# A fused two-layer gated cross-attention block: step tables of its own for the opening, and expert weights of both kinds streamed tile by tile

## The reference, cut to what matters

```
x = x + tanh(g_x[0]) * A(layernorm(x))    # one head of 256, additive mask [8,512,1601]
x = x + tanh(g_f[0]) * B(layernorm(x))    # self-attention, top 4 of 16 heads of 64, chosen per batch
x = x + tanh(g_x[1]) * C(layernorm(x))    # 16 heads of 16 on the context, integer mask [512,1601]
x = x + tanh(g_f[1]) * D(layernorm(x))    # 8 experts, 256->1024->256, one per token:
    h = relu(x_n @ W1[e] + b1[e]);  y = h @ W2[e] + b2[e];  out = y * route_p
```

## Time and profile before

| what | us |
|---|---|
| median of the 3 runs | 3057.81 |
| lowest and highest run | 3052.07, 3067.73 |
| the profiled execution, its own time | 3067.29 |
| its span, first to last instruction | 3065.5 |

### The profile page before, as it was taken

How to read it: one execution, slowest core, us unless ns; L and a number is a source line. 1 busy time by engine, 2 the same in 40 slices (tenths; PEclk the granted TensorE clock), 3 DMA queues, 4 the chain that set the end, 5 groups by cost and what they waited for, 6 DMA issues and landing times.

```text
span 3065.5 us, 39733 instructions
## 1 busy us (share of the span) xinstructions
PE 2738.2 (89%) x13624; PEld 1286.6 (42%) x13624; DVE 1742.3 (57%) x4230; ACT 1460.1 (48%) x2922; POOL 302.8 (10%) x352
## 2 busy tenths in 40 slices
PE   5767999899999998999899999999899879968998
PEld 2433343344333433343334333433343323228998
DVE  1336566566666666667666675666666767642111
ACT  2132356544654464546554555455545655632332
POOL 1200010002000200020001000110011000002222
PEclk9878999999999999999999999999999999978999
DMA  4213231323122403231222214231323022046664
GB/s 168 88 32 106 55 96 38 102 49 108 45 84 53 124 17 101 56 102 46 79 78 78 69 39 107 65 87 38 102 57 81 17 60 61 17 135 214 225 216 144
DMA packets 182901, 263.87 MB, mean 86 GB/s; under 512 B 50037, under 2 KB 148573, under 8 KB 182694
## 3 DMA queue, kind: packets, MB, share of 16 engines
q1 hardware_dynamic: 166188, 188.99, 23.3%
q0 software_dynamic: 16512, 72.32, 6.9%
HBM read 200.36 MB, written 60.50 MB: 85 GB/s over the span
## 4 chain that ended last, share of the span: by engine, by line
PE 77%; DVE 9%; issue 5%; ACT 5%; DMA 1%; SPq 1%; POOL 0%; ACTq 0%; POOLq 0%; DVEq 0%
PE PS L1295 13%; PE PS L1251 11%; PE PS L1278 10%; DVE mxC L1752 6%; PE PS L980 6%; PE PS L955 6%; PE PS L1419 5%; PE PS L1430 4%; PE PS L1003 3%; PE PS L1139 3%; PE PS L1048 2%; PE PS L1066 2%; PE PS L1058 2%; ACT reg L878 2%; PE PS L968 2%
## 5 line engine op out<-in xcount | busy, mean ns | idle before, releaser
L878 ACT ACTIVATE reg<-PS 128x512 f32<-128x512 f32 (+1 forms) x1664 | 966.6, 597 | 1073.6 <-PE PS L1278 1067.9
L1752 DVE TENSOR_REDUCE mxC<-PS 128x1 f32<-128x400 f32 (+1 forms) x2048 | 1101.5, 570 | 615.5 <-PE PS L1251 603.0
L1251 PE MATMUL PS<-reg 96*128 96x400 bf16 (+1 forms) x2048 | 670.7, 343 | 98.9 <-DVE mxC L1752 55.5
L1278 PE MATMUL PS<-reg 99*128 99x512 bf16 (+1 forms) x1664 | 618.9, 389 | 38.1 <-ACT reg L878 33.2
L1251 PEld LDWEIGHTS PS<-reg 96*128 96x128 bf16 x2048 | 193.2, 98 | 650.4 <-DVE mxC L1752 479.8
L1295 PE MATMUL PS<-reg 128*17 128x512 f32 (+1 forms) x3328 | 446.1, 609 | 0.0
L1278 PEld LDWEIGHTS PS<-reg 99*128 99x128 bf16 (+1 forms) x1664 | 163.6, 100 | 371.6 <-ACT reg L878 230.0
L955 PE MATMUL PS<-reg 128*128 128x512 f32 (+1 forms) x512 | 219.2, 536 | 6.3 <-issue 4.0
L980 PE MATMUL PS<-reg 128*128 128x512 f32 (+1 forms) x416 | 213.6, 606 | 0.4 <-ACT reg L752 0.4
L901 ACT ACTIVATE reg<-PS,reg 128x128 f32<-128x128 f32 x312 | 89.0, 368 | 215.9 <-PE PS L1419 207.7
L1419 PEld LDWEIGHTS PS<-reg 128*128 128x128 f32 x1248 | 147.7, 194 | 3.1 <-issue 1.0
(11 more groups left out here) (214 smaller groups left out, 2567.1 us busy)
## 6 DMA issues: line engine op xcount, KB each, us to landing
reg<-in_D_W SPq DMA_DIRECT2D x47, 1024.0 KB, 5.6
reg<-in_A_mask POOLq DMA_DIRECT2D x32, 800.5 KB, 5.3
dramK<-reg SPq DMA_DIRECT2D x144, 100.0 KB
dramV<-reg SPq DMA_DIRECT2D x48, 272.0 KB, 2.1
reg<-in_ctxT POOLq DMA_DIRECT2D x8, 1601.0 KB, 9.9
reg<-in_ctx POOLq DMA_DIRECT2D x8, 1536.0 KB, 7.7
dramQ<-reg SPq DMA_DIRECT2D x96, 128.0 KB
reg<-dramQ SPq DMA_DIRECT2D x32, 384.0 KB, 6.5
```

Of the source, the lines that this page charges most:

```text
L878: act.activation(pr[u % RING][0:r, :], PS[0:r, s_bank(v), :], ACT.Exp).then_inc(a_expC, 1)
L1251: last = mm(PS[:, bank, 0:w], qs[(NG * bb + g) % 3][0:ROWS, h, t * P:(t + 1) * P], ks[g % 2][0:ROWS, h, c0:c0 + w], start=True, stop=True)
L1278: last = mm(PS[0:r, bank, :], ks[g % 2][0:STK, h, c * P:c * P + r], qs[(NG * b + g) % 3][0:STK, h, :], start=True, stop=not with_mask)
L1752: v.tensor_reduce(mxC[:, h, t, j:j + 1], PS[:, m_ring(bb, g)[i % len(m_ring(bb, g))], 0:M_CH[j][1]], AX.X, ALU.max).then_inc(v_mx, 1)
```

## The change

It has two parts.

**The opening** gets a loop of its own, `for w in range(W_END)` with 226 steps, on every engine, and the main loop starts at b = 0. The functions `prepare` and `start_next` take a plan `p` in place of the global tables: `LOOP` holds the old tables, `FIRST` those of batch 0 and `SECOND` those of stage A of batch 1. Batch 0 uses other banks: a ring of four (MB, F0, F1) for stage A's scores, two for every set of transposes (F2 and SB[0]), MB for K and SB for V projections, four (F0, F1, MB) for stage B's scores; group 0 of C's first scores of batch 0 uses a ring of four (MB, SB). Stage A of batch 0 has four mask buffers, two of them in the region of `pr`, all loaded at the start. The K and V weights are loaded first with a semaphore of their own, the other 14 weight DMAs wait until mask row block 1 has landed, and PE waits for them only in `out_a`. Two K and three V chunks are projected before the router, the other ten chunks between the router and the B projections. `gather_heads` reads the four indices in one go and issues the four large DMAs, then the four small ones. `set_mask` moves to step 40, in stage A of batch 0, and `partition_all_reduce` behind batch 1's root. Stage A of batch 1 does its first eight chunks before or right behind C's Q projection, and C's first scores come after that, two per step in 32 steps.

**Stage D** keeps no W2 in SBUF: each tile loads W1, b1, W2 (1 MB) and b2 from SP in this order into one of WB = 6 buffers, with a semaphore for W1 and b1 and one for W2 and b2. The early load of all eight W2 and the registers `chosen` go.

```
-WB = 4
+WB = 6
+FIRST = Plan(SC=49, OA=(75, 77), LB=79, XB=(86, 88), RL=92, K=[78, 80, 94, 96, 98, 99, 100, 101],
+             V=[79, 81, 82, 90, 93, 95, 97], QB=(104, 105), KB=(106, 107), VB=(108, 109), LA=0, XA=(7, 9),
+             SB=O_SB, TB=[O_SB[i // 2] + 6 + 2 * (i % 2) for i in range(16)], PVB=(O_SB[3] + 11, O_SB[7] + 11),
+             OB=(150, 151), LC=153, QG=(10, 12), XC=(161, 163), QC=(165, 167),
+             S=[14, 15, 16, 17, 18, 19, 20, 21, 26, 27, 28, 29, 34, 35, 36, 37],
+             T=[22, 23, 24, 25, 30, 31, 32, 33, 38, 39, 40, 41, 43, 44, 45, 46],
+             PV=[48 + c for c in range(2 * CT)], wrap=0, ctx=0)
+SECOND = FIRST._replace(LA=100, XA=(112, 115), QG=(153, 155),
+                        S=[168, 170, 172, 174] + [178 + 10 * t + d for t in range(3) for d in (0, 2, 4, 6)],
+                        T=[178 + 10 * t + 2 * j for t in range(QT) for j in range(4)],
+                        PV=[216 + c for c in range(sum(u < NU for u in U_PV))], ctx=180)
+W_PIECE, W_ROWS = (186, 218), 222
+W_END = 226
...
 def m_ring(bb, g):
+    if bb == 0 and g == 0:
+        return MB + SB
...
+def ring_a(n, i):
+    return (MB + (F0, F1))[i % 4] if n == 0 else (F0, F1)[i % 2]
+def turn_a_bank(n, i):
+    return (F2, SB[0])[i % 2] if n == 0 else F2
+def k_bank(n, u):
+    return (MB if n == 0 else (F0, F1))[u % 2]
+def v_bank(n, i):
+    return (SB if n == 0 else (F1, F0))[i % 2]
+def ring_b(n, i):
+    return ((F0, F1), MB)[i // 2 % 2][i % 2] if n == 0 else (F0, F1)[i % 2]
...
-        w2 = take([NE, FM, D], F32)
+        w2 = [take([FM, D], F32) for _ in range(WB)]
...
+                    (wkC[:], a["C_WkT"]...), (wvC[:], a["C_WvT"]...), (bkC[:], a["C_bk"])):
+                sp.dma_start(dst, src).then_inc(ld["k"], 16)
+            sp.wait_ge(ld["mk1"], 16)
...
-                for j in range(ACTIVE):
-                    h = sp.value_load(rti[0:1, 1, j:j + 1], min_val=0, max_val=HB - 1)
+                _, heads = nc.values_load_multi_w_load_instructions(
+                    rti[0:1, 1, 0:ACTIVE], engines=[mybir.EngineType.SP], ...)
+                for j, h in enumerate(heads):
                     sp.dma_start(ws[:, :, :, j, :], a["B_w"][bass.ds(h, 1)]...)
...
+            for w in range(W_END):
+                bring(0, w, FIRST)
+                if w == 106:
+                    load_k(0, 0, 0)
+                    load_k(0, 0, 1)
+                    load_k(0, 1, 0)
+                    load_v(0, 0, N_LO, vc_lo)
+                if w == 178:
+                    load_q(0, 1)
...
-                             ).then_inc(w_loaded[par], 16)
+                             ).then_inc(w1_loaded[par], 16)
                 sp.dma_start(b1[par], ...)
+                sp.dma_start(w2[par], a["D_W2"][bass.ds(e, 1)].rearrange("o (k p) n -> p (o k) n", p=P)
+                             ).then_inc(w2_loaded[par], 16)
                 sp.dma_start(b2[par], ...)
...
             def project_k(n, u, piece):
-                if u == 0:
+                if n == 0:
+                    pe.wait_ge(ld["k"], 16 * NK)
+                    pe.wait_ge(v_ttr, 16)
+                    past(pe, v_kr, u - 1)
...
             def score_b(n, k):
-                if k == 0:
+                if n == 0 and k < 2:
+                    pe.wait_ge(v_qB, 2)
+                    pe.wait_ge(a_kB, 2)
+                elif n == 0:
+                    pe.wait_ge(a_expB, 2 * k - 2)
...
             def outputs(j):
+                pe.wait_ge(w2_loaded[j % WB], 32 * (j // WB + 1))
...
-                                  w2[:, bass.ds(chosen[j], 1), m, :].rearrange("p o n -> p (o n)"),
+                        last = mm(PS[:, 6 + (NH * j + t) % 2, 0:D], hT[:, m, t * P:(t + 1) * P], w2[j % WB][:, m, :],
```

More of the change, by code:

```diff
@@ L1 @@
+from collections import namedtuple
 from contextlib import ExitStack
@@ L256, in flamingo @@
         pr = [take([S], F32) for _ in range(RING)]
+        at = 2 * GH * C // 2 + 3 * GH * S // 2
+        eA0 = eA + [regC[:, at + i * C:at + (i + 1) * C] for i in range(2)]
         maskT = take([CT, S], BF16)
@@ L398, in gather_heads @@
                 sp.nop(nofuse=True)
-                for j in range(ACTIVE):
-                    h = sp.value_load(rti[0:1, 1, j:j + 1], min_val=0, max_val=HB - 1)
+                _, heads = nc.values_load_multi_w_load_instructions(
+                    rti[0:1, 1, 0:ACTIVE], engines=[mybir.EngineType.SP], min_val=0, max_val=HB - 1,
+                    skip_runtime_bounds_check_because="these are positions among the HB values of a row")
+                for j, h in enumerate(heads):
                     sp.dma_start(ws[:, :, :, j, :], a["B_w"][bass.ds(h, 1)].rearrange("o p m k n -> (o p) m k n")
                                  ).then_inc(ld["ws"], 16)
+                for j, h in enumerate(heads):
                     q = DB * (j % 2)
@@ L527, in _ @@
                     fill(b, u)
-                    if b == -1 and u == 100:
-                        sp.wait_ge(v_mT, 2)
-                        for i in range(2):
-                            sp.dma_start(ks[i][ROWS:STK, :, :], a["ones"].rearrange("r (h c) -> r h c", h=GH)
-                                         ).then_inc(ld["ones"], 16)
             def load_weights(j):
@@ L1353, in step, with open_step @@
                     scores_c(nb, ng, i, with_mask)
+            def open_step(w, with_mask=False):
+                prepare(0, w, FIRST)
+                start_next(0, w, FIRST)
+                start_next(1, w, SECOND)
+                if W_PIECE[0] <= w < W_PIECE[1]:
+                    for i in (2 * (w - W_PIECE[0]), 2 * (w - W_PIECE[0]) + 1):
+                        scores_c(0, 0, i, with_mask)
+                if w == W_ROWS:
+                    transpose_m(0, 0)
             def attend(with_mask):
-                for u in range((NG - 1) * UN, NU):
-                    step(-1, u, with_mask)
+                for w in range(W_PIECE[0], W_END):
+                    open_step(w, with_mask)
                 for b in range(B):
@@ L1360, in attend @@
                         step(b, u, with_mask)
-            for u in range(NU):
-                start_next(0, u)
-            for u in range((NG - 1) * UN):
-                step(-1, u, False)
+            for w in range(W_PIECE[0]):
+                open_step(w)
             pe.wait_ge(v_mf, 1)
@@ L1383, in _ @@
             last.then_inc(pe_rank, 1)
-            pe.wait_ge(v_tex, 1)
-            chosen = []
-            for j in range(0, ET, 8):
-                _, some = nc.values_load_multi_w_load_instructions(
-                    tex[0:1, j:min(j + 8, ET)], engines=[mybir.EngineType.PE], min_val=0, max_val=NE - 1,
-                    skip_runtime_bounds_check_because="the vector engine takes the minimum with NE - 1")
-                chosen += some
             for i in range(NT):
@@ L1835, in _, with nothing @@
             v.tensor_scalar(gA[:], PS[:, 0:KD, 0:D], 1.0 / 16.0, None, ALU.mult).then_inc(v_set, 1)
-            for b in range(-2, B + 1):
+            def nothing():
+                pass
+            for w in range(W_END):
+                prepare(0, w, FIRST, nothing)
+                start_next(0, w, FIRST, nothing)
+                start_next(1, w, SECOND, nothing)
+                if W_PIECE[0] <= w < W_PIECE[1]:
+                    for i in (2 * (w - W_PIECE[0]), 2 * (w - W_PIECE[0]) + 1):
+                        maxima(0, 0, i)
+                if w == W_PIECE[1]:
+                    split_m(0, 0)
+                if w == 40:
+                    set_mask()
+                if w == 44:
+                    set_gains()
+                if w == 136:
+                    set_flag()
+            for b in range(B + 1):
                 for u in range(NU):
```

436 lines of the change are left out of this document (246 added, 190 removed).

## The result

The changed kernel has a median of 3011.0 us over 4 runs (3007.19 to 3014.38), against 3057.9 for the kernel before in the same session: ratio 0.984, 95% interval 0.982 to 0.986. That is faster, by 1.6%. The forecast was 2997 in a range of 2976 to 3028: the sign and the range hold, the size is 14 us short. The profiled execution took 3012.11 with a span of 3010.4, at a mean granted clock of 0.972 against 0.965 before.

The account below looks back on a forecast made before the run. The prediction took PE, kept waiting or at reduced clock in the opening, as the bound. Opening steps summed to -66, say -65, stage D +4: -61, 3006 against the profiled 3067.3; less 9.5 for the median, 2997, range 2976 to 3028.

Parts of the forecast that it names:

- Step 7: Move to stage C, 224.5 to 244.1: QG covers part of the layer norm, PE idles some 2 us; -3.
- step 5: 164.8 to 172.7: PE's wait for batch 1's root behind POOL's all-reduce goes, the all-reduce moving to step 118; -7.9.
- Step 2: Stage A's scores, 37.3 to 79.9: more banks and masks leave 2.6 us idle; -8, between 0 and -10.7.
- Step 3: Weighing and out_a, 79.9 to 109.9: same work, so 0; a table load of about a microsecond possible.
- Step 8: C's Q parts through DRAM, 244.1 to 260.5: the branch, 4.05 of issue, now follows the wait; +1.5.
- Step 6: Stage B, 172.7 to 224.5: four score banks leave ACT binding, 38 us; -14, between 0 and -20.
- Step 4: K, V, B projections, 109.9 to 164.8: chunks cover waits, K stores queue behind the gather, 3.7 idle left; -12.
- Step 9: Maxima, 260.5 to 317.4: ring of four leaves a third of DVE's 14.9 us wait; -9, between 0 and -15.
- Stage D's +4: Streamed W2 at 340 GB/s makes a tile 7.65 us against PE's 7.26; +4, or 0 at 384 GB/s.
- The opening gives half: Rival: freed banks show the next wait, K stores on SP or ACT's list; -39, 3019 us; chance 0.24.
- W2 adds itself in full: Rival: stage D's DMA gaps can't be filled, a tile costs 10.3 us; +102, net +37, 3095; chance 0.03.
- PE's clock in stage D: Rival: DMA waits in every tile put one tile in four at half clock; +65, net 0, 3058; chance 0.03.

Follow-up runs that it names:

- Experiment 5: The changed kernel with one throwaway addition on POOL (the dummy) right behind the all-reduce; 3016.4 us.
- experiment 7: The changed kernel with the four small bias loads of batch 0's head gather issued after K chunk 3's store; 3013.2 us.
- extra_half: The changed kernel with each stage D tile loading half of its W2 once more into a buffer nobody reads; 3058.9 us.
- experiment 9: The changed kernel with the second tile's weights, too, waiting until the first tile's gathered rows are in; 3015.9 us.
- d_only: The kernel before with only stage D changed (W2 streamed, six buffers); 3062.99 us, ratio 1.000.
- experiment 10: The changed kernel run once more without edits, 3007.1 us, and best, 3004.2 us; its table compares the maxima stretch and mask wait across profiles.
- best: The changed kernel with branch at step 160, all-reduce plus throwaway at step 50, small gather loads later, second weight set held for gathered rows; 3004.2 us, ratio 0.982.
- best_mask: best with POOL issuing batch 1's context load after mask tile 2 instead of ahead of it; 2990.9 us, ratio 0.977.
- open_only: The changed kernel with stage D as before (eight W2 loaded once, WB = 4); 3011.09 us, ratio 0.982.

## Why the prediction was right or wrong

**What held.** The gain is in front, and stage D doesn't give it back; faster was right, and all landmarks up to 170 us came within 5 us: transposes at 14.1 (said 14), weighing at 62.3 (58), stage B's scores at 133.4 (131), end of the second weighing 169.1 (170). The opening gave 54.6 of the 66 forecast, with the first `scores_t` at 262.8 instead of 252. By steps, each as the difference between the lengths of the same stretch:

```
step                              forecast   measured
1 start                            -13.6      -13.8
2 scores of A                       -8.1       -3.8
3 weighing and out_a                 0         -3.0
4, 5 K, V, B projections, root     -19.9      -18.7
6 stage B                          -14        -16.1
7 move to C                         -3         +4.1
8 Q parts and branch                +1.5       +3.5
9 maxima                            -9         -6.8
sum                                -66        -54.6
```

**Step 7 failed, and through it a sentence of step 5.** Step 5 said that the all-reduce moves to step 118, "where nothing on POOL is needed for long". I took the 7.05 us of "issue" in the earlier trace rows for a cost that stands at the all-reduce and is over there. Experiment 5 shows it in two parts: 8.4 before the all-reduce, and 7.3 to 10.1 at the next tensor instruction on POOL, however much later. What the earlier trace rows had caught was the second part. In the changed kernel that instruction is the root of C's layer norm, and PE stands 6.26 for it, where the forecast had some 2. With the dummy, PE gets from stage B's output to the Q projection 4.5 us sooner: most of the 7.1 us by which step 7 was off. In the rest is a Q projection with PE at half clock (0.59 over its last 8.8 us).

**Step 2** was a size: I left 2.6 us idle and PE has 5.9 (32.93 busy of 38.80), at 0.91 where before it had 0.95. Step 3, counted as the same work, came in 3.0 shorter: the same 69 matmuls took 26.29 us at a clock of 1.00 instead of 29.31 at 0.90. **Step 8** was a size: 4.05 of branch became 5.75. **Step 6** was better than said. Its reasoning, that ACT binds, fits (busy 21.7 of 35.7 us), but no run took work from ACT, so it stays argued. **Step 4** left 3.7 of idle where 6.05 stand in one wait; the mechanism named there, K stores behind the gather, is the one in the trace, and experiment 7 shows that its small loads are 1 to 2 us of it. **Step 9** missed the mask on POOL, which was late next. DVE waited 1.5 us for it in the profile that is 2.2 short of the forecast, and 2.4 in the one that is 5 short; whether that is the whole miss isn't shown. The prediction should have listed it, because the change moved the maxima next to that load.

**Stage D's +4** came out as +3.3, by another way; that the two numbers agree is luck. The rate of 340 GB/s was too low: with the DMA share at 1.00 the trace shows 353 GB/s over the stretch including its drained end, and 368 in `extra_half` where DMA binds. 2.60 MB at 368 GB/s are 7.07 us, under PE's 7.26. The Trainium skill ("DMA: Bandwidth & Descriptors", Specifications) gives about 358 GB/s and so said "unchanged", which is what happened; taken as a ceiling, its figure is 3% below what the experiment moved. The +3.1 stands ahead of the tiles, at "the chain to the first tile runs through DVE's sort, so 0". The chain does run through the sort, but its last link is a row gather by DMA, and two tiles' weights with their W2 were put in front of it (experiment 9).

**From the profile to the median.** The sum was made against one profiled execution of 3067.3, 9.5 above the median, and I carried that offset over whole. The two profiles differ by 55.2, the two medians by 46.9. So of the 14 us between forecast and result, 6 are the sum's (-61 for -55) and 8 are this offset: the profile of before was a slower execution than its median, and that of after was near its own. The maxima aren't where the first lost its time: they take 56.9 us in it and 57.1 in `d_only`, the same code ahead of stage D, whose first `scores_t` is 3.1 us earlier and whose loop is 5.5 shorter (2394.6).

**The rivals.** "The opening gives half" (3019) is nearer the result than the forecast is, by 8 us against 14; in the opening's gain, 43 us against 65 where 54.6 were measured, the two are equally far. It had the mechanism for a part: a freed bank showed the next wait, though on POOL, not on SP or ACT. "W2 adds itself in full" and "PE's clock in stage D" are refuted by `d_only` and, for the second, by `extra_half`. The loop of wait and slow restart that the Trainium skill describes ("TensorE: Matmul & The Clock Gate", HAM oscillation) didn't start there, with 30 waits of up to 2.3 us at a mean clock of 0.98; no run here has longer waits in every tile.

**What stays open.** The stretch of the maxima takes 50 to 57 us with the same instructions, and its clock goes with the wait for the mask (the table of experiment 10; in `best` and `best_mask` the same matmuls took 44.95 and 39.44 us). What makes that wait 1.5 us in one profile and 4.4 in another is only seen in part: in `open_only` the mask was issued 1.2 us later, and PE did the four stage A matmuls ahead of the wait in 2.88 us instead of 3.62 and so came to it earlier. Why PE came back to full clock sooner there isn't shown. The 3.8 us of the loop are open too.

## What to carry to other kernels

Before costing a moved step at nothing, list what becomes the last condition at its new place, on every in-order queue: here four edits that removed visible waits brought 7 us together, not clear of the spread, and moving one mask load past a context load that was waiting for something else brought 13 more, so that the ratio went from 0.984 to 0.977, some 20 us. This kernel's all-reduce on POOL has a second half that falls on the next tensor instruction; put one there that nobody waits for. And take an opening's gain from medians or from several profiles, since the same program placed its stages up to 3 us apart, and profiles of the same opening had the first `scores_t` up to 7 us apart.

## What the runs showed of the hardware

- POOL's all-reduce had 8.35 and 8.42 us of "issue" before it (5.61 in the kernel before), and the next tensor instruction on POOL had 7.05 to 10.11; in the changed kernel two mask loads issued in between did not take this over.
- A branch cost PE 5.75 us in the changed kernel (4.8 to 5.6 in the others with its opening), 4.05 before.
- DMA moved 353 GB/s over 274 us with PE at full clock beside it, and 368 GB/s where it was the bound. Its slices in stage D of the changed kernel (40 equal slices, GB/s):

```profile
GB/s 316 382 376 371 377 370 379 372 374 372 376 365 380 377 378 374 375 371 375 375 373 376 379 375 375 373 376 378 374 375 366 375 373 375 375 371 371 286 19 22
```

- The clock fell behind a wait: after PE's 9.40 us of idle in `best` (experiment 10) two matmuls of C's first scores took 1.00 us, and two ahead of it 0.51; four of stage A took 1.88 ahead of it, three 2.76 behind it. That is the step between the two levels of 2.4 and 1.2 GHz:

```profile
201.18 1.88 PE L1072 MATMUL PS<-reg 128*128 128x512 f32 x4
203.33 0.51 PE L1399 MATMUL PS<-reg 96*128 96x400 bf16 x2
214.03 2.76 PE L1072 MATMUL PS<-reg 128*128 128x512 f32 x3
```
